# One kernel of eight GNN and FFN stages on Trainium2: the routed experts' second product in a K of 128 and four row groups, the conditioned norms on two row groups, and the edge layers' rows stored and loaded in another order

## The reference, cut to what matters

```
h = relu(h_src + edge_attr @ We[l] + be[l]);  agg = segment_sum(h, dst)          # L1_gnn
xn = (x - mu) * rsqrt(var + eps);  y = xn * (1 + cond @ sw + sb) + (cond @ bw + bb)  # L2_gnn norm
g = xf @ Wg[e];  u = xf @ Wu[e];  h = silu(g) * u;  y_e = h @ Wd[e]              # L2_ffn, h is 160 wide
```

## Time and profile before

| | us |
|---|---|
| median of three runs | 2763.17 |
| the profiled execution | 2755.71 |
| its span | 2753.9 |
| TensorE busy | 2547.8 (93%) |
| VectorE busy | 1170.4 (42%) |
| ScalarE busy | 756.7 (27%) |
| GpSimd busy | 726.5 (26%) |

### The profile page before, as it was taken

How to read it: one execution, slowest core, us unless ns; L and a number is a source line. 1 busy time by engine, 2 the same in 40 slices (tenths; PEclk the granted TensorE clock), 3 DMA queues, 4 the chain that set the end, 5 groups by cost and what they waited for, 6 DMA issues and landing times. The chain is left out here.

```text
span 2753.9 us, 33974 instructions
## 1 busy us (share of the span) xinstructions
PE 2547.8 (93%) x11318; PEld 1689.3 (61%) x11318; DVE 1170.4 (42%) x2661; ACT 756.7 (27%) x1487; POOL 726.5 (26%) x717
## 2 busy tenths in 40 slices
PE   4798869989989998899999999999999999789997
PEld 3465437757757655475665766766666666457774
DVE  9713955535535555353343442635222222530001
ACT  0522333323423322153251441521211121111121
POOL 0541955425425400001001010112344443101110
PEclk9898979999989998899999999999999999889998
DMA  3111045435335330110201100102999875548885
GB/s 83 43 55 61 12 136 156 117 123 154 110 122 150 114 128 12 42 46 28 78 1 52 54 21 31 47 19 80 309 288 284 236 220 166 112 160 313 316 288 175
DMA packets 91466, 340.21 MB, mean 124 GB/s; under 512 B 28528, under 2 KB 28656, under 8 KB 83114
## 3 DMA queue, kind: packets, MB, share of 16 engines
q1 hardware_dynamic: 50855, 245.90, 27.7%
q0 software_dynamic: 40448, 92.15, 11.6%
HBM read 338.59 MB, written 36.52 MB: 136 GB/s over the span
## 5 line engine op out<-in xcount | busy, mean ns | idle before, releaser
L84 PE MATMUL ps<-W,HT 128*128 128x320 f32 (+3 forms) x1432 | 533.6, 513 | 2.4 <-ACT HT L2450 1.5
L84 PEld LDWEIGHTS ps<-W,HT 128*128 128x128 f32 (+2 forms) x1432 | 256.5, 190 | 166.3 <-issue 115.2
L84 PE MATMUL ps<-XT,W 128*128 128x250 f32 (+1 forms) x1184 | 326.4, 431 | 2.8 <-ACT XT L1250 1.6
L84 PEld LDWEIGHTS ps<-XT,W 128*128 128x128 f32 x1184 | 225.3, 192 | 100.5 <-issue 17.5
L1028 PE MATMUL ps<-XN,W 128*128 128x512 f32 x504 | 263.6, 606 | 4.2 <-ACT GT L1302 3.5
L1627 POOL TENSOR_TENSOR H<-H,RB 125x512 f32<-125x512 f32 x40 | 50.7, 1267 | 749.8 <-DVE XN L1956 749.8
L2305 POOL DMA_INDIRECT result_rows<-KT,LOGC x110 | 112.6, 1024 | 460.2 <-DVE KT L2484 221.0
L84 PEld LDWEIGHTS ps<-HT,W 128*128 128x128 f32 x1152 | 133.8, 195 | 9.3 <-issue 8.1
L1004 POOL DMA_INDIRECT QT<-node_rows,LOGC x84 | 79.7, 949 | 210.3 <-DMA node_rows<-V 149.9
L1138 PEld LDWEIGHTS ps<-P,QT 128*128 128x128 f32 x672 | 91.0, 197 | 71.5 <-issue 71.5
L84 PE MATMUL ps<-HT,W 128*128 128x128 f32 x1152 | 134.1, 278 | 0.8 <-DVE HT L2902 0.8
(11 more groups left out here) (570 smaller groups left out, 4276.4 us busy)
## 6 DMA issues: line engine op xcount, KB each, us to landing
W<-in_L_ffn_w SPq DMA_DIRECT2D x38, 2048.0 KB, 7.4
W<-in_L_ffn_Wgu SPq DMA_DIRECT2D x92, 640.0 KB
W<-in_L_ffn_Wd SPq DMA_DIRECT2D x92, 320.0 KB
W<-in_L_gnn_Wqkv SPq DMA_DIRECT2D x4, 3072.0 KB, 10.1
W<-in_L_gnn_W SPq DMA_DIRECT2D x5, 2048.0 KB, 24.4
W<-in_L_gnn_Wm SPq DMA_DIRECT2D x4, 2048.0 KB, 7.9
W<-result_rows SPq DMA_DIRECT2D x5, 1344.0 KB
RB<-in_L_gnn_rows SPq DMA_DIRECT2D x24, 256.0 KB, 3.5
```

Of the source, the lines that this page charges most:

```text
L84: last = nc.tensor.matmul(out, lhs(k), rhs(k), start=(k == 0), stop=(k == nk - 1))
```

## The change

1. **Routed experts.** The hidden 160 is split in 128 and 32. VectorE writes the 128 into one of four tiles and the 32 into a quarter of a tile that four slots share. Each slot has one transpose and one matmul of K 128 (`down`, which raises `d_mm`). Once in four slots, in iteration 4g + 5, there is one transpose of the shared tile (`rest_transposed`) and, at the end of the iteration, four matmuls of K 32 on row groups 0, 32, 64 and 96, into four PSUM banks (`rest_down`, which raises `y_mm`). VectorE's copy of a result moves from iteration sl + 2 to the head of iteration sl + 6. The weights ring has 8 places, the 320 KB come as 128 and 32 rows in two DMAs, and loads wait for `d_mm` of the slot 8 before. The PSUM of the transposed rows has one bank instead of two. GpSimd's loop is as it was, with 8 gather buffers.
2. **Norms.** Scale weights lie in partitions 0 to 16 and bias weights in 32 to 48, the condition is made twice (64 columns in place of 16 in `embed`), and the two matmuls of `cond` have a K of 32 on row groups 0 and 32. Each load of the weights is two DMAs.
3. **Edge layers.** A store of V is two DMAs, of 112 and 13 rows. The loads into RB and of `L1_gnn_W12` wait until 12 slots of the layer have had their ReLU. The H row of tile t - 1 is written after the statistics of tile t. One copy on GpSimd at the stage's start is gone.

```diff
@@ l1_gnn_block, sync
-                    sp.dma_start(hb[t * R:(t + 1) * R, :], b.V[0:R, t, :]).then_inc(s["hb_stored"], 16)
+                    for lo, hi in PARTS:
+                        sp.dma_start(hb[t * R + lo:t * R + hi, :], b.V[lo:hi, t, :]).then_inc(s["hb_stored"], 16)
+                sp.wait_ge(s["relu_ready"], NSLOT * layer + GR)
@@ l1_gnn_block, vector, last tiles of a layer
-                        finished(layer, t - 1)
+                        stored_rows(layer, t - 1)
+                        if layer == NL - 1:
+                            finished(layer, t - 1)
...
+                    if t and layer < NL - 1:
+                        finished(layer, t - 1)
+                stored_rows(layer, T - 1)
                 finished(layer, T - 1)
@@ l2_gnn_block, cond
-                    last = nc.tensor.matmul(b.ps[0:R, 6 + a, :], b.GT[:, t * R:(t + 1) * R],
-                                            b.affine[n][:, a * D:(a + 1) * D], start=True, stop=True)
+                    last = nc.tensor.matmul(b.ps[0:R, 6 + a, :], b.GT[32 * a:32 * a + 32, t * R:(t + 1) * R],
+                                            b.affine[n][32 * a:32 * a + 32, a * D:(a + 1) * D], start=True, stop=True,
+                                            tile_position=(32 * a, 0))
@@ l2_routed_blocks, sync
-                    sp.wait_ge(s["y_mm"], sl - WR + 1)
+                    sp.wait_ge(s["d_mm"], sl - WR + 1)
+                if sl >= 4 * RR:
+                    sp.wait_ge(s["y_mm"], 4 * (sl // 4 - RR + 1))
@@ l2_routed_blocks, tensor
             def down(sl):
                 pe.wait_ge(s["ht_ready"], sl + 1)
-                if sl >= 2:
-                    pe.wait_ge(s["copied"], sl - 1)
-                matmul_rows(nc, b.ps[:, 6 + sl % 2, :], lambda k: hT[sl % 2][:, k, :],
-                            lambda k: Wd[sl % WR][:, k, :], 2).then_inc(s["y_mm"], 1)
+                if sl >= 4:
+                    pe.wait_ge(s["copied"], sl - 3)
+                nc.tensor.matmul(b.ps[:, 4 + sl % 4, :], hT[sl % 4], r.w_down[sl % WR], start=True, stop=False)\
+                    .then_inc(s["d_mm"], 1)
+            def rest_down(g):
+                pe.wait_ge(s["rest_ready"], g + 1)
+                pe.wait_ge(r.rest_in[g % RR], 64 * (g // RR + 1))
+                for q in range(4):
+                    group = slice(32 * q, 32 * q + 32)
+                    nc.tensor.matmul(b.ps[:, 4 + q, :], restT[g % 2][group], r.w_rest[g % RR][group], start=False, stop=True,
+                                     tile_position=(32 * q, 0)).then_inc(s["y_mm"], 1)
             for sl in range(NS + 2):
...
+                if sl >= 5 and sl % 4 == 1:
+                    rest_transposed(sl // 4 - 1)
...
+                if sl >= 5 and sl % 4 == 1:
+                    rest_down(sl // 4 - 1)
@@ l2_routed_blocks, vector
-            for sl in range(NS + 2):
+            for sl in range(NS + 6):
+                if sl >= 6:
+                    q = sl - 6
+                    dve.wait_ge(s["y_mm"], 4 * (q // 4 + 1))
+                    if q >= YR:
+                        dve.wait_ge(scattered[q % YR], 16 * (q // YR))
+                    v.tensor_scalar(b.result[q % YR][:, :], b.ps[:, 4 + q % 4, :], 1.0, None, ALU.mult).then_inc(s["copied"], 1)
...
-                if 0 <= sl - 2 < NS:
-                    q = sl - 2
-                    dve.wait_ge(s["y_mm"], q + 1)
-                    if q >= YR:
-                        dve.wait_ge(scattered[q % YR], 16 * (q // YR))
-                    v.tensor_scalar(b.result[q % YR][:, :], b.ps[:, 6 + q % 2, :], 1.0, None, ALU.mult).then_inc(s["copied"], 1)
```

More of the change, by code:

```diff
@@ L997, in _ @@
         def _(pool):
-            nc.gpsimd.tensor_copy(b.GT[0:32, :], b.ident[0:32, 16:17].to_broadcast([32, NP])).then_inc(s["ones"], 1)
             for layer in range(NL):
-                pool.wait_ge(s["hb_stored"], 16 * T * (layer + 1))
+                pool.wait_ge(s["hb_stored"], 32 * T * (layer + 1))
                 for t in range(NSLOT):
@@ L1063, in final, with embed @@
                     .then_inc(s["wf_mm"], 1)
-            def embed(w, rhs, done):
-                matmul_columns(nc, b.slot(1), 16, lambda k: w, lambda k: rhs, 1).then_inc(s[done], 1)
+            def embed(w, rhs, m, done):
+                matmul_columns(nc, b.slot(1), m, lambda k: w, lambda k: rhs, 1).then_inc(s[done], 1)
             def normed_turned(t):
@@ L1300, in _ @@
                     act.wait_ge(s["cond_mm"], 1)
-                    act.wait_ge(s["ones"], 1)
-                    nc.scalar.activation(halves(b.GT[0:16, :]), b.slot(1)[0:16, :, 0:HF], ACT.Identity,
-                                         bias=b.cols[0:16, C["f_b2"]:C["f_b2"] + 1]).then_inc(s["cond"], 1)
+                    nc.scalar.activation(halves(b.GT[0:64, :]), b.slot(1)[0:64, :, 0:HF], ACT.Identity,
+                                         bias=b.cols[0:64, C["f_b2"]:C["f_b2"] + 1]).then_inc(s["cond"], 1)
             turned_out(2)
@@ L1353, in finished @@
                                            ALU.add).then_inc(s["hb_ready"], 1)
+            def finished(layer, t):
+                if layer < NL - 1:
                     dve.wait_ge(s["hb_ready"], T * (layer + 1) + t + 1)
@@ L2417, in hidden_transposed @@
             def hidden_transposed(sl):
[L2418 to L2422, removed]
-                                               hid[sl % 2][:, q * HC:(q + 1) * HC], b.ident[:, :])
-                last.then_inc(s["h_mm"], 1)
+                pe.wait_ge(s["h_ready"], 2 * (sl + 1))
@@ L3075, in pad, with twice @@
         return out
+    def twice(x, next_row):
+        out = np.zeros(64, f)
+        for at in (0, 32):
+            out[at:at + 16], out[at + 16] = x, next_row
+        return out
     freq = pad(np.tile(np.arange(1, 33, dtype=f) * f(TWO_PI / 16), 2))
     cols = [col(a["L0_gnn_b1"]), col(a["L0_gnn_g1"]), col(a["L0_gnn_be1"]), col(a["L0_gnn_b2"]), col(a["L0_gnn_g2"]),
-            col(a["L0_gnn_be2"]), a["L0_ffn_b1"].T, freq, pad(a["L2_gnn_f_b1"]), pad(a["L2_gnn_f_b2"])]
+            col(a["L0_gnn_be2"]), a["L0_ffn_b1"].T, freq, pad(a["L2_gnn_f_b1"]),
+            pad(twice(a["L2_gnn_f_b2"], f(1)))]
     out = {
@@ L3098, in _layout @@
         "L1_ffn_w2": np.concatenate(list(a["L1_ffn_w2"]), axis=1),
-        "L2_gnn_f_w1": a["L2_gnn_f_w1"], "L2_gnn_f_w2": a["L2_gnn_f_w2"],
+        "L2_gnn_f_w1": a["L2_gnn_f_w1"], "L2_gnn_f_w2": np.stack([twice(x, f(0)) for x in a["L2_gnn_f_w2"]]),
         "L2_gnn_sb": np.concatenate([np.concatenate([a[f"L2_gnn_{n}_w"], a[f"L2_gnn_{n}_b"][:, None, :]], axis=1)
```

109 lines of the change are left out of this document (69 added, 40 removed).

## The result

The changed kernel takes 2835.54 us (median; 2831.32 to 2848.97), the kernel before, run beside it, 2763.73: ratio 1.0269, 95% interval 1.0234 to 1.0303. The profiled execution took 2835.73 us, span 2834.0.

The account below looks back on a forecast made before the run. TensorE's order of work was taken to set the time nearly everywhere. Late gather +150, clock +63, change 2 -6 and change 3 -17 summed to +190 on 2763.17: 2953 us, range 2845 to 3060.

Parts of the forecast that it names:

- The added wait: Routed experts: the late copy delays scatter and gather, TensorE waits; four slots take 26.6 and 23.4 us, not 18.12; +141.
- L: A routed gather's time from issue to landing: 5.5 us for slots with rows, 3.9 for empty ones, bounds 10.9 and 2.1.
- The rest product in the link of every fourth slot: Routed experts: slot 4g's copy waits for the four rest matmuls, put at 2.15 us; two iterations take 9.0 + L.
- the five passes: Rest product, routed experts: a second pass blocks the queue, so the four matmuls on row groups take 2.15 us.
- The clock: Routed experts: gaps twice in four slots lower TensorE's clock, 3.0 us per group; +63 for 21 groups, between 0 and 181.
- the other link: Routed experts, slots 4g + 1 to 4g + 3: from copy through scatter to gather, two iterations take 6.6 + L.
- Head and tail: Routed experts: iteration 7 starts 2.6 us later; one rest product and four copies and scatters at the end add 6.
- Change 2: Norms, third GNN: four passes of `cond` become three less 0.26 for the switch, 0.17 for each of 40; -6 us.
- Change 3: Edge layers' boundaries: moved loads let gathers land sooner, -14; two DMAs per store, -3; sum -17, bounds -5 and -24.
- The rival with the other sign: Routed experts: the gather lands in time and TensorE never waits; DMA-bound first half gains nothing; 2725 us, chance 0.05.
- the short link: Routed experts, slots 4g + 1 to 4g + 3: two iterations take 6.6 + L; gave the rival's threshold L = 2.5.
- the long link: Routed experts, slot 4g, whose copy waits for the rest matmuls: two iterations take 9.0 + L.

Follow-up runs that it names:

- gather_ahead: The changed kernel with GpSimd issuing the gather of slot sl + 8 before the scatter of slot sl - 4 in the routed experts: 2681.41 us, ratio 0.9704.
- before_late: The kernel before with an added GpSimd wait ahead of each routed-experts scatter, so scatter and next gather come about as late as in the changed kernel: 2941.48 us, ratio 1.0639.
- gather_ahead_2: gather_ahead run once more, on the same chip as loads_early_2: 2683.35 us, ratio 0.9715.
- loads_early_2: gather_ahead without SyncE's wait for 12 ReLUs, so the moved loads go out ahead of the first gathers again: 2682.28 us, ratio 0.9710.

## Why the prediction was right in direction and wrong in size

Direction, place and mechanism came as forecast. The size failed: for change 1 I had 213 us (150 and 63), and from the stage's first matmul to the next stage's first it is 94.0. The landing time and the rest product in the chain were too long, and the clock's cost was the largest error.

- *The added wait.* Right as a mechanism, shown from both sides by gather_ahead and before_late. Over the 21 groups the trace has 476.8 us: ten with rows of 20.9 to 28.3, mean 24.1, eleven empty of 18.7 to 27.2, mean 21.5. I had 523 + 63 = 586. Three terms failed:
  - *L.* From issue to landing the gathers took 4.4 us in the mean in slots with rows and 3.5 in empty ones, not 5.5 and 3.9. I took the shortest gather seen in the earlier trace rows, but most of these had full DMA engines beside them; at a share of 0.67 and 0.55 they were shorter. 10 x 2 x 1.1 + 11 x 2 x 0.4 = 31 us too much.
  - *The rest product in the link of every fourth slot.* 1.08, not 2.15: 21 x 1.07 = 22 us too much. The step that failed is "The second pass of a group needs the rows of its first, so I let it start with the first pass of the next group", the five passes. The records show the first passes of two groups starting at 1198.874 and 1198.880, the second passes at 1199.405 and 1199.411: in `cond` the second group's first pass does not wait for the first group's second one. The eight passes of the rest product run alike, four starts from 1959.385 to 1959.405 and four from 1959.918 to 1959.938. So in the link of every fourth slot two iterations take 7.9 + L, not 9.0 + L; in the other link 6.5 + L, where I had 6.6.
  - *The clock.* +63 forecast. 523 - 31 - 22 = 470, so only 476.8 - 470 = 7 us are left for it. By the windows above the lower level was granted for some 0.2 x 215 + 0.04 x 270 = 54 us, in eleven stretches, not in twice 21. At half the clock 54 us can cost 27 at most, so +63 was out of reach whatever the other terms were. The gaps came out mostly at 1 to 4 us, not 3 to 4.6, since L and the rest product were shorter, and part of what was slow fell into time that was waited out anyway (the last point is argued, not shown). The level itself was read right from the earlier trace rows; the step that failed is carrying one gap's price over to 42 gaps. In before_late, where the gaps are regular, the clock did cost over 3 us for each group (27.4 and 26.5 against 23.9 and 23.2), near my 3.0.
- *Head and tail.* +2.6 and +6 forecast. From the stage's first matmul to that of the next stage are 420.9 us before and 514.9 after; the 21 groups (382.4 and 476.8) take all of the 94.0, so nothing is left.
- *Change 2.* -6 forecast, -13.1 measured, 0.33 for each of 40. From the first pass to the next matmul `cond` takes
```profile
1198.87 1.12 PE L1667 MATMUL ps<-W,GT 32*125 32x512 f32 x4
1199.93 1.32 PE L92 MATMUL ps<-KT,QT 128*125 128x313 f32 x4
```
1.06 us in the changed kernel; four passes of 0.43 were 1.72. Two passes plus 0.2 for the way in and out is what it costs, not three plus 0.26. The sum over a stage is half of 40 x 0.66; where the rest goes I did not find.
- *Change 3.* -17 forecast, -5.8 measured. The first add came as forecast; the step that failed was to count its lead as the layer's. On a chip with the stop the moved loads (-14 forecast) gave nothing (gather_ahead_2 against loads_early_2), and the stores in two parts, put at -3, brought the gathers 11 us forward, of which part was lost behind the stop. On the chip without the stop the moved loads are worth 17 us or more.
- *The rival with the other sign.* "The gather is not late" was priced at 2725. gather_ahead is that kernel, at 2681: "the first half is bound by the DMA engines, which are full already, and gains nothing" was wrong. It gained as much for each slot as the second half, (18.13 - 15.58) / 4 = 0.64, where I had 0.34, since the rest product is short. Its threshold (L = 2.5) was also taken from the short link alone. In the long link the two iterations take 8.46 us in gather_ahead, against 7.9 + L in the changed kernel, so with GpSimd's loop as it was this gather is late from L = 0.5 on, and none landed under 2.1.

In the Trainium skill, "TensorEngine Tiling (Array Packing)", Key Properties, a switch of tiling mode drains the engine. The trace puts a small price on it: four slots of gather_ahead take 15.58, of which 4 x 3.56 + 0.11 + 0.86 = 15.21 are passes, so both switches and what the overlap lacks together cost 0.37 (an estimate from these starts).

## What to carry to other kernels

When a result is collected over several steps, look at what else stands in the queue that hands it on: here a gather four slots ahead lost its lead because it stood behind a scatter, and putting it first turned +3% into -3%. A busy DMA share of 1 was no limit in bytes here, and the landing time of a transfer has to be taken at the load of the new kernel, not of the old one. A gain at the head of a chain counts only up to the next thing that ends late, so follow it to the steady state before adding it up.

## What the hardware showed that I had not expected

- Float32 matmuls on four row groups (32 rows each, 512 columns) took 1.08 us for eight passes, 3.63 in one group.
- 3.6 us of matmuls on 32 rows alone, without a pause, were followed by matmuls at half the clock in 13 of 21 groups (one run); four row groups side by side in gather_ahead never were (clock 1.00 throughout).
- With 256 of the 320 KB of a slot's second weights in 128 rows of 2 KB the DMA engines moved 340 GB/s at a share of 0.98, with all of it in 80 rows of 4 KB 291 at 1.01. No run separates the layout from the rest of change 1.
- A store of 125 rows in two DMAs of 112 and 13 rows let the gathers start 3.3 us after the last V row's start instead of 5.9.
- On three of four sets of runs a VectorE add at the start of each edge layer stood still, mostly until a burst of 12 gathers had been out for some 3.2 us (17.0 us after the first), on one never: 690.9 against 718.3 us for the same code of that stage.
